# Weight splits: high parts on Pool, low parts on VectorE, weights one slot further from their splits

## The reference

```python
xp = einsum('ntd,dh->nth', x, Wx) + b                  # x: (2, 1024, 256)
h_t = tanh(xp_t + h_{t-1} @ Wh)                        # 1024 steps, h0 = cond_1024
shared = silu(h @ shared_w1.T) @ shared_w2.T           # 256 -> 1024 -> 256
gates = softmax of the top 2 of h @ gate_w.T           # 8 experts
expert_out[e] = silu(h @ experts_w1[e].T) @ experts_w2[e].T
out = x + shared + sum over the two chosen experts of gate * expert_out
```

## Time and profile before

| | |
|---|---|
| median of 3 runs | 381.51 us (381.47 to 382.41) |
| the profiled execution | 381.38 us, its span 379.7 us |
| TensorE busy | 356.2 us (94%) |
| ScalarE busy | 244.1 us (64%) |
| VectorE busy | 200.2 us (53%) |
| Pool busy | 108.5 us (29%) |
| rounds 1 and 2 | 28 to 79.5 us of the span |
| first FFN matmul | 80.25 us |

### The profile page before, as it was taken

The page is one execution under the profiler, slowest core; times in us unless marked ns, Lnnn a source line. Parts: engine busy times, 40 slices in busy tenths (PEclk is TensorE's granted clock), DMA queues, the critical chain, the costliest instruction groups (busy, mean ns, idle before and its releaser), DMA issues.

```text
span 379.7 us, 8904 instructions
## 1 busy us (share of the span) xinstructions
PE 356.2 (94%) x2458; PEld 253.0 (67%) x2459; DVE 200.2 (53%) x415; ACT 244.1 (64%) x478; POOL 108.5 (29%) x99
## 2 busy tenths in 40 slices
PE   5989999997997998999999999999999999999981
PEld 4758889964664675666667666667766666666660
DVE  0089999979996988964333323333323333232310
ACT  3777788888556778865555665556665556665530
POOL 1100010000276788600123333223333133332241
PEclk9999999999999999999999999999999999999996
DMA  6999999607697979999898998889988989989992
GB/s 194 422 421 434 428 407 334 194 4 124 87 199 182 225 180 226 235 194 196 176 129 153 168 155 155 147 149 156 158 149 154 148 142 158 148 159 147 152 127 28
DMA packets 158173, 73.50 MB, mean 194 GB/s; under 512 B 140736, under 2 KB 155200, under 8 KB 156992
## 3 DMA queue, kind: packets, MB, share of 16 engines
q1 hardware_dynamic: 146672, 59.83, 66.9%
q0 software_dynamic: 6864, 9.11, 16.9%
q10 hardware_dynamic: 4608, 4.20, 4.1%
HBM read 23.68 MB, written 16.53 MB: 106 GB/s over the span
## 4 chain that ended last, share of the span: by engine, by line
PE 80%; ACT 6%; DMA 5%; issue 3%; DVE 2%; another core or an unknown queue 1%; ACTq 1%; POOL 0%; SPq 0%; DVEq 0%; POOLq 0%
PE py L1138 32%; PE z L1033 30%; PE z L1047 8%; PE z L982 3%; PE z L1014 3%; DMA space<-recurrence_w 2%; DMA space<-space 2%; ACT space L799 1%; ACT space L876 1%; PE px L1025 1%; PE py L982 1%; PE z L995 1%; DMA space<-x_cols 1%; ACTq L896 1%
## 5 line engine op out<-in xcount | busy, mean ns | idle before, releaser
L1138 PE MATMUL py<-w_slots,space 128*128 (+1 forms) x1272 | 148.4, 273 | 7.4 <-DMA space<-recurrence_w 3.7
L1033 PE MATMUL z<-w_slots,x 128*128 (+1 forms) x636 | 145.9, 379 | 0.8 <-issue 0.8
L1138 PEld LDWEIGHTS py<-w_slots,space 128*128 128x128 f16 x1272 | 123.8, 98 | 33.1 <-issue 3.5
L1033 PEld LDWEIGHTS z<-w_slots,x 128*128 128x128 f16 x636 | 62.1, 98 | 65.0 <-issue 1.2
L453 POOL DMA_INDIRECT out<-space x37 | 57.5, 1553 | 157.0 <-issue 65.2
L876 ACT ACTIVATE space<-z,tile_scales 128x512 f32<-128x512 f32 x106 | 71.8, 678 | 41.3 <-PE z L1033 34.1
L582 DVE SCALAR_TENSOR_TENSOR recurrence_w<-space,tile_scales,recurrence_w 128x512 f16<-128x512 f32 x54 | 40.5, 750 | 71.7 <-ACT recurrence_w L881 65.6
L582 DVE SCALAR_TENSOR_TENSOR space<-space,tile_scales 128x512 f16<-128x512 f32 x52 | 39.0, 750 | 57.7 <-ACT space L881 42.4
L528 DVE SCALAR_TENSOR_TENSOR w_slots<-w_slots,w_scale 128x1024 f16<-128x1024 f32 x36 | 46.2, 1283 | 1.3 <-issue 0.3
L881 ACT ACTIVATE recurrence_w<-space,tile_scales 128x512 f16<-128x512 f32 x54 | 39.0, 722 | 8.7 <-ACT space L876 2.5
L430 POOL DMA_INDIRECT sorted_rows<-space x32 | 39.1, 1221 | 17.5 <-issue 13.1
(11 more groups left out here) (114 smaller groups left out, 178.9 us busy)
## 6 DMA issues: line engine op xcount, KB each, us to landing
w_slots<-weights SPq DMA_DIRECT2D x9, 2048.0 KB, 30.5
sorted_rows<-pad_row SPq DMA_DIRECT2D x1, 5070.0 KB, 60.2
space<-x_rows ACTq DMA_DIRECT2D x16, 128.0 KB
out<-space ACTq DMA_DIRECT2D x16, 128.0 KB
space<-x_cols SPq DMA_DIRECT2D x1, 1024.0 KB, 8.6
space<-recurrence_w SPq DMA_TRANSPOSE x54
space<-space SPq DMA_TRANSPOSE x52
x<-sorted_rows SPq DMA_TRANSPOSE x39
```

What stands on the lines that cost most here:

```text
L1033: last = nc.tensor.matmul(Z[u % 2][h][:], x16[:, u, x_part, k], weight(f, k * HID + h * BANK, BANK, part), start=k == 0 and x_part == 0 an ...
L1138: last = nc.tensor.matmul(PY[p][:, 0:D], hiddenT[:, p, low, q], weight(f, MATRIX + q * D, D, part), start=q == 0 and not low and part == 0 ...
```

## The change

High parts of pieces 0 to 27 (FFNs 0 to 6) move from VectorE to Pool (`split_high`), which makes them batch by batch behind each reduce; it waits for the scales by a new semaphore `scaled`, and VectorE's low part waits for `high_by_pool`. The weights lie 3 slots behind their place, so high part c only waits for low part c - 2. VectorE makes 28 low parts ahead of `states_low(0)`, and searches FFNs 4 and 5, behind pieces 11 and 15; ScalarE searches FFNs 6 and 7 in round 2, 512 columns in a step. Batches are five instead of six. Of the last 8 pieces ScalarE makes the high part and VectorE the low part, one in each tile g = 6 to 13; nothing is split in tile g = 3.

```diff
-SPACE = 2 * K * NTOK + 2 * HID - 512
+SPACE = 2 * K * NTOK + HID
-EARLY_WIDES = 6 * WIDES - 2
+AHEAD_SLOTS = 3
+EARLY_WIDES = 7 * WIDES
-BOUND_BATCHES = ((0, 2), (2, 3), (3, 4), (4, 5), (5, 6), (6, FFNS))
+BOUND_BATCHES = ((0, 2), (2, 3), (3, 5), (5, 7), (7, FFNS))
 FOUND_BY_DVE = BOUND_BATCHES[0][1]
-WIDE_FINDS_FROM = FOUND_BY_DVE + L // CHUNKS
+GAP_FINDS = {11: FOUND_BY_DVE + L // CHUNKS, 15: FOUND_BY_DVE + L // CHUNKS + 1}
+LATE_FINDS_FROM = max(GAP_FINDS.values()) + 1
 SPLIT_FROM = 6
-LATE_WIDES = BOUND_BATCHES[-1][0] * WIDES
-LATE_SPLITS = tuple(range(LATE_WIDES + (3 * n + 1) // 2, LATE_WIDES + (3 * n + 4) // 2) for n in range(TILES - 2 - SPLIT_FROM))
+FOUND_BEFORE = (None, CHUNKS, 2 * CHUNKS, 3 * CHUNKS, 4 * CHUNKS + WIDES)
+BOUNDS_BEFORE = (2, 2, 3, 4, 4)
...
-            return w_slots[:, 2 * c + 2:2 * c + 4].rearrange("p s c -> p (s c)"), high, low, w_scale[:, f, m:m + 1]
+            return w_slots[:, 2 * c + AHEAD_SLOTS:2 * c + AHEAD_SLOTS + 2].rearrange("p s c -> p (s c)"), high, low, w_scale[:, f, m:m + 1]
...
-            for n in range(len(BOUND_BATCHES) - 1):
+            def split_high(c):
+
+                whole, high, low, scale = wide(c)
+                if c >= 2:
+                    pool.wait_ge(split_ok, c - 1)
+                nc.gpsimd.tensor_scalar(high, whole, scale, None, ALU.mult).then_inc(high_by_pool, 1)
+
+            for n, (first, end) in enumerate(BOUND_BATCHES[:-1]):
                 reduce_bounds(n)
+                pool.wait_ge(scaled, n + 1)
+                for f in range(first, end):
+                    pool.wait_ge(w_in[f], 16)
+                for c in range(first * WIDES, end * WIDES):
+                    split_high(c)
             reduce_bounds(len(BOUND_BATCHES) - 1)
...
-            nc.vector.memset(chunk_bound[:, WIDE_FINDS_FROM:], 0.0).then_inc(bound_ok, 1)
+            nc.vector.memset(chunk_bound[:, LAST], 0.0).then_inc(bound_ok, 1)
...
-            def split(c, high_by_act=False):
+            def split_low(c, ready, count):
 
                 whole, high, low, scale = wide(c)
                 if c:
                     dve.wait_ge(split_ok, c)
-                if high_by_act:
-                    dve.wait_ge(high_ok, highs_by_act.index(c) + 1)
-                else:
-                    link(nc.vector.tensor_scalar(high, whole, scale, None, ALU.mult))
+                dve.wait_ge(ready, count)
                 nc.vector.scalar_tensor_tensor(low, whole, scale, high, ALU.mult, ALU.subtract).then_inc(split_ok, 1)
...
-            split_upto(FOUND_BY_DVE * WIDES)
-            for n in range(1, len(BOUND_BATCHES) - 1):
+            for n, (first, end) in enumerate(BOUND_BATCHES[:-1]):
                 find_scales(n)
-                split_upto(min(BOUND_BATCHES[n][1] * WIDES, EARLY_WIDES))
+                dve.sem_inc(scaled, 1)
+                if n == 0:
+                    link(nc.vector.tensor_copy(tile_scales[:, 0:TILES].rearrange("p t s -> p s t"),
+                                               ffn_scales[:, :, 0:1].broadcast_to([P, 3, TILES])))
+                for c in range(first * WIDES, end * WIDES):
+                    split_low(c, high_by_pool, c + 1)
+                    if c in GAP_FINDS:
+                        find_largest(GAP_FINDS[c]).then_inc(bound_ok, 1)
...
-                elif g < TILES - 2:
-                    if g == 3:
-                        split_upto(LATE_WIDES)
-                    elif g == 4:
-                        find_scales(5)
-                        route_tiles()
-                    elif g == 5:
-                        route_scales()
+                elif g == 4:
+                    find_scales(len(BOUND_BATCHES) - 1)
+                    dve.sem_inc(scaled, 1)
+                    route_tiles()
+                elif g == 5:
+                    route_scales()
                 if g >= AHEAD:
                     shared_y(g - AHEAD)
                 if SPLIT_FROM <= g < TILES - 2:
-                    for c in LATE_SPLITS[g - SPLIT_FROM]:
-                        split(c, high_by_act=c in highs_by_act)
+                    split_low(EARLY_WIDES + g - SPLIT_FROM, high_by_act, g - SPLIT_FROM + 1)
...
             for r in range(1, SPECULATIVE_ROUNDS):
-                chunks = 1 if r == 1 else 2
-                first_found = FOUND_BY_DVE if r == 1 else WIDE_FINDS_FROM
+                first_found = FOUND_BY_DVE if r == 1 else LATE_FINDS_FROM
...
                 if SPLIT_FROM <= g < TILES - 2:
-                    c = highs_by_act[g - SPLIT_FROM]
+                    c = EARLY_WIDES + g - SPLIT_FROM
                     whole, high, low, scale = wide(c)
-                    act.wait_ge(split_ok, c)
-                    nc.scalar.mul(high, whole, scale).then_inc(high_ok, 1)
+                    act.wait_ge(scaled, len(BOUND_BATCHES))
+                    act.wait_ge(split_ok, c - 1)
+                    nc.scalar.mul(high, whole, scale).then_inc(high_by_act, 1)
```

## The result

The changed kernel takes 469.0 us (median, 466.1 to 470.1), the kernel before 382.0 us measured beside it: 1.223 times the time, 95% interval 1.217 to 1.229. The forecast was 407.5 us with a range of 392 to 428. The sign was right, and the size was off by a factor of 3.3: +87 us instead of +26. Two steps carry the miss: changes between kinds of instructions on Pool, which the sum held at nothing (38 us), and the price of Pool's multiply (18 us).

A forecast was written before the change was run, and what follows sets the result against it. TensorE, busy 94% of the span, bounds the kernel, and VectorE's early list fixes the FFN's start: 381.4 + 26.6 (later states_low(0)) + 1.0 (clock) - 1.5 (late stage) = 407.5 us, range 392 to 428.

The forecast's parts named there:

- Which wait ends last: Seam between recurrence and FFN: VectorE's early list fixes the start of states_low(0), moving it from 79.68 to 106.3, +26.6 us.
- VectorE's own work: Early list: 28 low parts 37.2 us, two searches 8.9, three more sets of scales 3.4; alone ending at 78.6.
- rival (c): Early list: no hold between high and low parts, 1.33 us a piece, states_low(0) at 85.0, 386 us; chance 0.08.
- The price of a high part on Pool: Early list: Pool's multiply of 1024 elements taken at 1.15 us, from bounds by memsets and the affine select.
- The changes of kind: Pool between reduces and high parts: only 1.26 us of scales and semaphore after a reduce, nothing for switching instructions.
- Turns at the port: Early list: Pool's high and VectorE's low parts take turns in both directions, 2.35 us a piece against 2.1.
- The rule on the lock: SBUF port of VectorE and Pool: an exclusive lock, the later instruction blocked altogether while the other holds it.
- Behind S: After the start of states_low(0): +1.0 us for TensorE's clock, -1.5 us given back in the late stage.
- The low clock: First FFN matmuls: TensorE restarts at its lower clock after 26 us without work, +1 us.
- The late stage: FFN tiles, 103 to 160 us: VectorE loses six highs and six lows, shortening waits on hidden-row transposes, -1.5 us.

The follow-up runs named there:

- r9: The kernel with plain copies as Pool's high parts, its 28 early low parts made from one SBUF input, without subtracting the high part: 389.8 us.
- r1: The changed kernel with each of Pool's five reduces over the partitions replaced by a plain copy on Pool: 430.8 us.
- r2: The changed kernel with the 28 high parts back on VectorE and everything else of the change kept: 408.2 us, 1.066 times before.
- r6: The changed kernel with Pool's high parts as plain copies from f32 to f16, the scale left out: 404.8 us.
- r3: The changed kernel with each of the first 28 low parts made as two instructions of 512 columns: 470.5 us.
- r7: The changed kernel with idle float32 matmuls on TensorE, nine behind each of the last eight early low parts: 466.5 us.

## Why the prediction was right, and where it failed

**Which wait ends last: right.** VectorE's early list sets S, and nothing else moved the start of the FFN. Round 2 gained nothing from the narrower search: TensorE's last work of the recurrence still ends at about 80 us.

**VectorE's own work: right.** 28 low parts of 1.33 us, two searches of 4.45 and three more sets of scales were the list. r9 has this list with only 3.8 us of waiting for Pool, and its S is 84.6, where rival (c), the same list without holds, said 85.0.

**The price of a high part on Pool: wrong, 18 us.** The step said 1.15 us, "since one multiply is less than a select and more than a write". It measured 2.83. With it the pace of a piece is Pool's alone, 2.83, instead of 2.35, and high parts on Pool cost S 23.4 us (r1 against r2) where the sum had 26.6 - 21.4 = 5.2. Of the 18.2 us between them, 28 x 0.48 = 13.4 are the pace; most of the rest is low parts of 1.28 us that now stand bare behind the last high part of each of the four batches (an estimate from r1's rows). The reasoning from neighbours failed: the affine select of the earlier trace rows costs at most 2.2 ns an element, the memset 0.86, the copy of r6 about 1.0, the multiply 2.5. Even the bound that counted no fixed cost, 2.26 us, was passed. The Trainium skill (GPSIMD Engine Reference, section "Performance versus the Vector engine") gives 1.03 cycles an element to bodies of up to two operations, which at the 1.2 GHz of its section "Specifications" would be 0.88 us for 1024 elements (an estimate). The copy's 1.04 us with its fixed cost is near that; the multiply's 2.5 ns an element is about three times as much.

**The changes of kind: not in the sum, 38 us.** This is the step that failed most: the sum puts 1.26 us of scales and semaphore between a reduce and the next high part, and nothing between a high part and the next reduce. A sign of it was in the rows: the affine select of the earlier trace rows stands behind 7.84 us of "issue", and I read the instruction and passed over the bracket. In r1, which has no reduce, the same select starts at 1.59 us without a gap, so the gap comes with the reduces in the program. In the kernel before, it is early and beside nothing that needs Pool. The change put Pool's reduces and multiplies in turns: eight changes of kind, six of them paid on the path. The Trainium skill (GPSIMD Engine Reference, section "Instruction dispatch") states that the first call to a freshly loaded kernel on Pool pays about 6 us behind a MODIFY_POOL_CONFIG; the rows agree in size, with 5.7 to 6.1 us (the gaps less 1.3 us where the scales are waited for), and show that it is paid anew at each alternation. The first change took 9.0 us, and why stays open. The DMA queues were busy with the weights then, but beside the second change, of 6.08 us, they were too (window rows as in the earlier trace rows):

```profile
27.00:33.00 6.00, 5.38 (x37) 4.49 (x38) 1.77 (x9) 3.67 (x14) 0.40 (x1) 1.00 1.01 431
61.10:67.00 5.90, 5.90 (x50) 5.75 (x49) 1.28 (x1) 3.81 (x14) 0.00 (x0) 1.00 1.09 333
```

**Turns at the port: right in kind, and for one duration right in size.** For a high part of about 1.15 us the step gave a period of 1.33 + 1.15 - 0.14; with the copy of 1.04 us it would be 2.23, and r6 measured 2.18. S there is 102.8 and the time 404.8 us, against a forecast of 407.5 with highs of 1.15, and 403 with 0.98. Rival (c), no hold, gave 85.0 and 386; r9, which takes the hold away, has 84.6 and 389.8. So had Pool's high part had the copy's price and come without changes of kind, the forecast would have stood; a cheap multiply alone would still have left the 38 us. With a multiply of 2.83 us the hold doesn't set the pace, since the low part, even stretched to 2.07, fits under the next high part. Here the step was wrong, and by luck in the other direction: full turns would have given a period of 1.33 + 2.83 - 0.14 = 4.02 us instead of 2.83, some 33 us more in 28 pieces (an estimate).

**The rule on the lock.** The rows show a hold in both directions. A high part that started at 118.73 us, 0.06 us behind the start of a low part, took 3.94 us instead of 2.83 (the two high parts from there took 6.76 us together):

```profile
118.67 1.29 DVE L531 SCALAR_TENSOR_TENSOR w_slots<-w_slots,w_scale 128x1024 f16<-128x1024 f32 x1
```

The 1.11 us more are about what was left of the low part, less Pool's fixed cost. The other way the hold is not the whole instruction: 0.79 us of a multiply of 2.83, 0.35 of one of 1.56, 0.86 of a copy of 1.04. The Trainium skill (SBUF — State Buffer, section "Who interferes with whom") has the later one wait for the whole instruction of the other. For the copy the two can't be told apart; for the multiply the measurement decides: VectorE was held for a first stretch, and ran beside the rest. That this stretch is the time in which Pool reads its input is my guess; no row shows when Pool reads.

**Behind S: half right.** The low clock was taken at +1 and measured 1.1. The late stage was to give back 1.5 us and took 4.4 instead (first down matmul to the end: 288.4 us before, 292.8 after). The step failed in its reason, that a lighter VectorE would shorten TensorE's waits for the turned hidden rows: TensorE's waits behind the first down matmul grew from 7.4 to 8.6 us, 1.2 more. And behind two of them the granted clock fell, which the sum did not have. Behind a wait of 2.43 us it stood at 0.50 for some 3.2 us of work, which costs about 1.6 (an estimate, half of that time); behind a wait of 2.00 us at the end the last 24 matmuls took 4.47 us instead of 3.32. These rows are the changed kernel's, the last that of the kernel before:

```profile
206.34 3.87 PE L1134 MATMUL py<-w_slots,space 128*128 128x256 f16 x20 [2.43 <-DMA space<-space]
207.00:208.00 1.00, 1.00 (x6) 0.67 (x5) 1.00 (x4) 0.82 (x2) 0.09 (x1) 0.50 1.88 173
455.06 4.47 PE L1134 MATMUL py<-w_slots,space 128*128 x24 [2.00 <-DMA space<-recurrence_w]
...
367.99 3.32 PE L1138 MATMUL py<-w_slots,space 128*128 x24 [1.48 <-DMA space<-recurrence_w]
```

Together that is 4 of the 4.4 us. What moves the waits stays open. With the same late stage the experiments range from 287.7 (r6) over 289.6 (r7) to 293.7 (r3), so it isn't the lighter VectorE that decides there. ScalarE stands for 4 to 9.5 us in sum on a releaser that is no engine of the core, as in the earlier trace rows, in all of these kernels but r7; but r6, with 8.3 us of it, has the shortest late stage, so it doesn't explain the differences by itself.

The sum of the misses: 18.2 (the high part's price) + 38.2 (changes of kind) + 6 (behind S) = 62, and 407.5 + 62 = 469.5.

## What to carry to other kernels

Before you give work to Pool, look at what Pool does just ahead and behind it: a change between kinds of its instructions can cost 6 us each way (here the reduce over partitions and the multiply), and on the timeline it stands only as idle time with no releaser. Price a Pool instruction from a run of that very instruction, since a copy and a multiply of the same bytes differed by 2.7 times. And a helper that reads SBUF beside a VectorE instruction with two SBUF inputs is no second pair of hands: even with the cheap copy and no changes of kind, a piece took 2.18 us on two engines, against 2.11 on one.

## What the runs showed of the hardware that I had not expected

- Pool's `tensor_scalar` multiply of 128x1024 f32: 2.83 us, 2.76 with a constant, 2.84 with f32 out, 0.3 us fixed and 2.5 ns an element. Its copy to f16: 1.04 us.
- Going from the reduce over partitions to this multiply, or back: 5.7 to 6.1 us each, 9.0 the first time; going from the reduce to the copy and back, or from the copy to the multiply and back: nothing.
- Pool holds VectorE's two-input instruction for 0.8 to 0.9 us per 1024 elements of its own instruction, at the start of it, whether that lasts 1.04 or 2.83 us.
- TensorE came back at 1.2 GHz after 83 us of rest and stayed there for some 5 us, at a cost of 1.1 us. The first matmuls were as slow after 4.8 us of rest (r9), and the granted clock also fell to 0.50 behind waits of 2.43 and 2.00 us in the FFN stage.
